# Layer 1 of a graph network: indices copied a group earlier, weights and a column row in PSUM, and a small POOL memset beside each gather

## What is computed

```python
def _L1_gnn_ref(x, W_u, b_u, W_v, src, dst):
    s_u = x @ W_u.T + b_u
    s_v = x @ W_v.T
    e = s_u[src] + s_v[dst]
    e = jnp.where(e >= 0, e, 0.2 * e)
    m = jax.ops.segment_max(e, dst, num_segments=n_nodes)
    e_exp = jnp.exp(e - m[dst])
    denom = jax.ops.segment_sum(e_exp, dst, num_segments=n_nodes)
    probs = e_exp / denom[dst]
    xh = x.reshape(n_nodes, head_dim, num_heads)
    msg = xh[src] * probs[:, None, :]
    out = jax.ops.segment_sum(msg, dst, num_segments=n_nodes)
    return out.reshape(n_nodes, dim)
...
x = _layernorm(x + _L0_gnn_ref(x, edge_index, edge_attr_64, ...), axis=-1)
x = _layernorm(x + _L1_gnn_ref(x, L1_gnn_W_u, L1_gnn_b_u, L1_gnn_W_v, src, dst), axis=-1)
```

## Time and profile before

| | us |
|---|---|
| median of three runs | 4930.07 |
| lowest, highest | 4929.89, 4938.38 |
| the profiled execution | 4929.81 |
| its span, first to last instruction | 4928.1 |

### The profile page before, as it was taken

One profiled execution on the slowest core, in us unless ns is written; L12 is line 12 of the kernel. 1 busy time (PEld: TensorE's weight loads), 2 busy tenths in 40 slices (PEclk: granted clock), 3 DMA queues, 4 the chain that ended last, 5 costly groups with the idle time before them and its releaser, 6 DMA issues. The chain is left out here.

```text
span 4928.1 us, 61408 instructions
## 1 busy us (share of the span) xinstructions
PE 3099.3 (63%) x13554; PEld 1900.6 (39%) x13555; DVE 2202.6 (45%) x5019; ACT 908.4 (18%) x2810; POOL 3434.9 (70%) x2948
## 2 busy tenths in 40 slices
PE   3547877777777777877778768834444444444441
PEld 1224444444444444444444435523333333333331
DVE  2543333333333333333333349855555555555554
ACT  0212222222222222222222223300000000000002
POOL 4238888888888888888888867756666666666564
PEclk9869898888998888888898889956666666666665
DMA  7777767667767677677677666643333333333332
GB/s 285 193 241 137 135 126 136 133 123 135 132 126 138 127 131 134 126 135 132 123 136 132 123 133 206 181 148 93 95 92 100 93 94 91 96 98 94 92 93 66
DMA packets 471760, 641.52 MB, mean 130 GB/s; under 512 B 173608, under 2 KB 365636, under 8 KB 467887
## 3 DMA queue, kind: packets, MB, share of 16 engines
q0 software_dynamic: 198144, 339.26, 36.4%
q1 hardware_dynamic: 245994, 254.83, 17.6%
q10 hardware_dynamic: 27588, 47.08, 3.0%
HBM read 448.23 MB, written 192.71 MB: 130 GB/s over the span
## 5 line engine op out<-in xcount | busy, mean ns | idle before, releaser
L935 POOL DMA_INDIRECT S<-l_msum,l_sink x784 | 1280.7, 1634 | 254.2 <-issue 213.5
L1466 POOL DMA_INDIRECT l_feats<-X_rows,l_gsrc x880 | 1008.1, 1146 | 605.6 <-DVE l_gsrc L1574 340.7
L918 POOL DMA_INDIRECT l_ga<-A_rows,l_gsrc x784 | 791.3, 1009 | 265.6 <-issue 155.4
L1008 PE MATMUL l_psU<-l_hid,l_same 128*128 128x257 f32 x1568 | 585.0, 458 | 534.7 <-ACT l_hid L1044 518.2
L981 PE MATMUL l_psC<-l_table,l_onehot 128*128 x4728 | 726.5, 295 | 0.0
L1532 PE MATMUL l_psU<-l_feats,l_same 128*128 128x264 f32 x1760 | 555.7, 481 | 146.5 <-DVE l_feats L1699 129.2
L1048 ACT COPY l_msum<-l_psU 128x257 f32<-128x257 f32 x784 | 292.6, 373 | 1883.8 <-POOLq L934 1296.1
L974 PE MATMUL l_psC<-W1cT,l_attrT 64*128 64x256 f32 x1576 | 619.0, 476 | 13.1 <-DMA l_table<-B_rows 13.1
L981 PEld LDWEIGHTS l_psC<-l_table,l_onehot 128*128 128x128 bf16 x4728 | 426.0, 104 | 364.9 <-issue 303.4
L1008 PEld LDWEIGHTS l_psU<-l_hid,l_same 128*128 128x128 f32 x1568 | 266.1, 213 | 669.9 <-ACT l_hid L1044 598.9
L1532 PEld LDWEIGHTS l_psU<-l_feats,l_same 128*128 128x128 f32 x1760 | 413.8, 242 | 281.8 <-issue 189.2
(11 more groups left out here) (346 smaller groups left out, 3512.2 us busy)
## 6 DMA issues: line engine op xcount, KB each, us to landing
l_srcb<-src_rows SPq DMA_DIRECT2D x99, 512.0 KB
l_locb<-lo_rows SPq DMA_DIRECT2D x55, 512.0 KB
S<-su_zeros ACTq DMA_DIRECT2D x24, 1156.5 KB
l_locb<-loc_rows SPq DMA_DIRECT2D x99, 256.0 KB
nd_sums<-S SPq DMA_DIRECT2D x196, 128.5 KB, 2.2
l_attr<-in_edge_attr SPq DMA_DIRECT2D x98, 256.0 KB
GH_rows<-l_hidden SPq DMA_DIRECT2D x49, 384.0 KB
nd_hidden<-GH_rows SPq DMA_DIRECT2D x49, 384.0 KB, 3.2
```

Of the source, the lines that this page charges most:

```text
L918: pool.indirect_dma_start(ga[:, s, :], None, D["A"], bass.IndirectOffsetOnAxis(ap=gsrc[h][:, j % HALF:j % HALF + 1], axis=0)).then_inc(gat ...
L935: pool.indirect_dma_start(D[f"S{j % NTAB}"], bass.IndirectOffsetOnAxis(ap=sink[j // HALF][:, j % HALF:j % HALF + 1], axis=0), msum[:, j % ...
L1008: nc.tensor.matmul(psU[j % 2][:, 0:UW], same[j // HALF][:, j % HALF, :], hid[:, j % RING, :], start=True, stop=True).then_inc(agg_done, 1)
L1466: pool.indirect_dma_start(feats[r][:, t, :], None, D["X1"], bass.IndirectOffsetOnAxis(ap=gsrc[r][:, t:t + 1], axis=0)).then_inc(gathered[r ...
```

## The change

- `stage_index(g + 2, r)` moves from the end of DVE's body g to its start.
- A new PSUM bank, `psW`, holds `weight` (128 columns) and `column` (128 columns). `K["column"]` is copied there once, ahead of the loop, and `find_edge` reads that copy.
- ACT takes the exponential of `below` twice: first into `weight` (`weights_ready`), then into `feats` as before (`weights_in_rows`). DVE multiplies by `weight`, and PE waits for `weights_in_rows` as well.
- POOL, in every body of `ahead` (53 groups), issues behind each gather a memset of the new tile `pause` (128 x 128 floats), which first waits for the memset before it.

```diff
--- before.py
+++ after.py
@@ -1383,11 +1383,13 @@
         goes_on = m.sb("goes_on", [P, XG])
         stays = m.sb("stays", [P, XG])
         xblock = m.sb("xblock", [1, XT])
+        pause = m.sb("pause", [P, P])
         word = m.sb("word", [1, XPACKED])
         words = m.sb("words", [1, XPACKED], I32)
         psE = m.ps("psE", [P, 512])
         psM = m.ps("psM", [P, 512])
         psV = m.ps("psV", [P, 512])
+        psW = m.ps("psW", [P, 512])
         psU = [m.ps(f"psU{q}", [P, 512]) for q in range(4)]
         keys_in, tables_ready, table_split = m.sem("keys_in"), m.sem("tables_ready"), m.sem("table_split")
         loc_in = [m.sem(f"loc_in{r}") for r in range(SETS)]
@@ -1399,12 +1401,15 @@
         ends_ready, ends_turned = m.sem("ends_ready"), m.sem("ends_turned")
         carries_ready, carries_turned, shrink_ready = m.sem("carries_ready"), m.sem("carries_turned"), m.sem("shrink_ready")
         max_ready, max_turned = m.sem("max_ready"), m.sem("max_turned")
-        below_ready, weights_ready = m.sem("below_ready"), m.sem("weights_ready")
+        below_ready, weights_ready, weights_in_rows = m.sem("below_ready"), m.sem("weights_ready"), m.sem("weights_in_rows")
         weighted, agg_done, acc_done = m.sem("weighted"), m.sem("agg_done"), m.sem("acc_done")
+        paused = m.sem("paused")
         dve_step, pool_waited = m.sem("dve_step"), m.sem("pool_waited")
         block = st.enter_context(nc.Block())
 
         ENDS, CARRY, SHRINK = P, P + 2 * GROUP, P
+        weight = psW[:, 0:GROUP * NH].rearrange("p (t h) -> p t h", h=NH)
+        column = psW[:, P:2 * P]
 
         def groups(engine, body):
 
@@ -1478,7 +1483,11 @@
                         pool.wait_ge(agg_done, g * PAIRS + (t + QUARTER) // PAIR)
                         pool.sem_inc(pool_waited, 1)
                     gather(r, t)
-
+                    pool.wait_ge(paused, g * GROUP + (t + 1))
+                    pool.sem_inc(pool_waited, 1)
+                    nc.gpsimd.memset(pause[:, :], 0.0).then_inc(paused, 1)
+
+            nc.gpsimd.memset(pause[:, :], 0.0).then_inc(paused, 1)
             ahead(pool, body)
             for r in range(SETS):
                 pool.wait_ge(gathered[r], 16 * GROUP * len(range(r, XG, SETS)))
@@ -1522,6 +1531,7 @@
                 pe.wait_ge(max_ready, g + 1)
                 nc.tensor.transpose(psM[:, 0:P], top[:, :], K["ident"][:, :]).then_inc(max_turned, 1)
                 pe.wait_ge(same_ready, g + 1)
+                pe.wait_ge(weights_in_rows, g + 1)
                 for n in range(PAIRS):
                     if n % 2 == 0:
                         pe.wait_ge(weighted, g * 4 + (n // 2 + 1))
@@ -1561,7 +1571,8 @@
                 act.wait_ge(carries_turned, g + 1)
                 nc.scalar.activation(shrink[:, :], psE[:, SHRINK:SHRINK + NH], ACT.Exp).then_inc(shrink_ready, 1)
                 act.wait_ge(below_ready, g + 1)
-                nc.scalar.activation(feats[r][:, :, H:XW], below[:, :, :], ACT.Exp).then_inc(weights_ready, 1)
+                nc.scalar.activation(weight, below[:, :, :], ACT.Exp).then_inc(weights_ready, 1)
+                nc.scalar.activation(feats[r][:, :, H:XW], below[:, :, :], ACT.Exp).then_inc(weights_in_rows, 1)
                 if not isinstance(g, int) or g < XG - SETS:
                     act.wait_ge(sv_done, g + 1)
                     stage_window(g + SETS, r)
@@ -1578,7 +1589,7 @@
                 nc.vector.tensor_scalar(onehot[:, :, :], locb[r][:, :, :], K["winid"][:, 0:1], None, ALU.is_equal).then_inc(onehot_ready, 1)
 
             def find_edge(g):
-                nc.vector.tensor_tensor(same[:, :, :], K["column"][:, :].unsqueeze(1).to_broadcast([P, GROUP, P]),
+                nc.vector.tensor_tensor(same[:, :, :], column.unsqueeze(1).to_broadcast([P, GROUP, P]),
                                         K["loX"][:, bass.ds(g * GROUP, GROUP)].unsqueeze(2).to_broadcast([P, GROUP, P]),
                                         ALU.is_equal).then_inc(same_ready, 1)
 
@@ -1627,6 +1638,7 @@
             split_float(nc, first_steps, K["svf"][:, :, :], svrest[:, :, :],
                         [table[:, :, n * NH:(n + 1) * NH] for n in range(NSPLIT)])
             dve.sem_inc(table_split, 1)
+            nc.vector.tensor_copy(column, K["column"][:, :])
             nc.vector.memset(ones[:, :], 1.0)
             nc.vector.memset(forth[:, 0:1], LOW)
             nc.vector.memset(carry[:, 1, GROUP - 1:GROUP], LOW)
@@ -1653,6 +1665,8 @@
                 c = Chain(dve, dve_step, base)
                 at = bass.ds(g * GROUP, GROUP)
 
+                if not isinstance(g, int) or g < XG - SETS:
+                    stage_index(g + SETS, r)
                 if not last:
                     find_node(g + 1, 1 - r)
                 if not first:
@@ -1693,9 +1707,8 @@
                     c.link(nc.vector.tensor_tensor(rows, rows, factor[:, :].unsqueeze(1).to_broadcast([P, XW // NH, NH]), ALU.mult))
                 dve.wait_ge(weights_ready, g + 1)
                 for q in range(4):
-                    f = feats[r][:, q * QUARTER:(q + 1) * QUARTER, :]
-                    f3 = f[:, :, 0:H].rearrange("p t (c h) -> p t c h", h=NH)
-                    w3 = f[:, :, H:XW].unsqueeze(2).to_broadcast([P, QUARTER, H // NH, NH])
+                    f3 = feats[r][:, q * QUARTER:(q + 1) * QUARTER, 0:H].rearrange("p t (c h) -> p t c h", h=NH)
+                    w3 = weight[:, q * QUARTER:(q + 1) * QUARTER, :].unsqueeze(2).to_broadcast([P, QUARTER, H // NH, NH])
                     nc.vector.tensor_tensor(f3, f3, w3, ALU.mult).then_inc(weighted, 1)
                     if q == 1 or q == 2:
                         add_sums(g, (2 * q - 2, 2 * q - 1), blocks, first)
@@ -1704,8 +1717,6 @@
                 if not last:
                     take_scores(g + 1, 1 - r, c)
                     local_max(g + 1, 1 - r, c)
-                if not isinstance(g, int) or g < XG - SETS:
-                    stage_index(g + SETS, r)
                 if first:
                     steps["first"] = c.n
                 elif "every" not in steps:
```

## The result

The changed kernel takes 4975.88 us, the median of 5 runs (4963.92 to 4982.53), against 4931.09 for the kernel before (5 runs). The ratio is 1.0083, with a 95% interval of 1.0065 to 1.0101: slower by 0.8%. Forecast were 4662 us, with 4570 to 4850 as the range.

What follows compares the result with a forecast made beforehand. The prediction took a ring of index list, gathers and scores, 28.97 us a group, to bound layer 1. Cut, POOL's 23.7 and DVE's 23.1 plus 0.3 jitter give 24.0 us, saving 268.4: 4662 us, range 4570 to 4850.

Steps and rivals of the forecast that it cites:

- The ring of index list, gathers and scores: Layer 1: POOL waits for DVE's index list, DVE for gathered rows, 28.97 us a group; copying a body earlier cuts it.
- the sum for the two chains and their jitter: Layer 1, per group: POOL 23.7 us, DVE 23.1, plus 0.3 for jitter passed between them, giving 24.0 us.
- The stretched gathers: POOL's gathers held up by DVE instructions with two SBUF inputs: 0.2 us each, 3.2 a group, of which about 0.5 stays.
- DVE's instructions on PSUM: DVE's `same` and weighting reading an operand in PSUM: priced at nothing, keeping 2.28 and 1.22 us.
- The memset: POOL, behind each of a group's 16 gathers: 0.20 us taken, between bounds of 0 and 0.50.
- The rival in which each gather starts anew: The memset and its wait empty POOL's sequencer, 0.92 us to each gather's start: 33.6 us a group, 5180 us; chance 0.08.
- the ring is cut, and what remains is the slower of two chains, POOL's and DVE's with PE: Layer 1 after the early index list: the slower chain sets the group time, POOL 23.7 us or DVE 23.1.
- DVE's chain: DVE with PE in layer 1, without the wait for gathered rows: 23.1 us a group.
- `agg_done` has come by the time POOL wants it: POOL between groups: sums of the group two before are finished before the next scores, so gathers run straight on.
- The rests that I struck from the bill: POOL's gathers: the surplus of 0.2 us each from stretching by DVE, of which 3.2 us a group shrinks to about 0.5.
- The rival on the far side of the sign: Slower than before: each gather starts anew behind its memset, 33.6 us a group, 5180 us; chance 0.08.

Runs made afterwards that it cites:

- h_reduces: b_index_only with DVE's edge-matrix comparison (all groups but the first) and weighting replaced by equally long reductions with one SBUF input, nothing in PSUM: 5017.37 us, ratio 1.0152.
- a_no_memset: The changed kernel without its memsets and their semaphore; early index list and PSUM operands stay: 5078.62 us, ratio 1.0282 to the kernel before.
- i_half_rows: a_no_memset with half the bytes in each gather (128 rows of 132 floats in place of 264): 5077.95 us, ratio 1.0291 to the kernel before.
- j_pause256: The changed kernel with memsets of 256 columns in place of 128: 4768.84 us, ratio 0.9662 to the kernel before.
- j_pause384: The changed kernel with memsets of 384 columns in place of 128: 4737.82 us, ratio 0.9603 to the kernel before.
- b_index_only: The kernel before with only the index list copy moved from the end of the body to its start: 4704.03 us, ratio 0.9515.
- l_every_second: b_index_only with a memset of 128 columns behind every second gather: 4665.59 us, ratio 0.9518, on a chip where the kernel before took 4901.51.
- c_psum_only: The kernel before with only weight and column in the new PSUM bank, index list late, no memset: 5142.47 us, ratio 1.0419.

## Why the prediction was wrong

- **The ring of index list, gathers and scores: right.** It bound the kernel, and the copy a body earlier cuts it. Alone it gives 24.66 us a group; the sum for the two chains and their jitter was 24.0 for the whole change.
- **The stretched gathers: right in cause and size.** They fell from 1146 to 969 ns, with 0.97 to 1.0 us forecast, and h_reduces shows the cause without PSUM: 958 ns as soon as DVE's long instructions have one SBUF input. The Trainium skill (SBUF — State Buffer, "Who interferes with whom") has VectorE instructions with two SBUF inputs collide with a GpSimd instruction that reads SBUF, and the trace agrees for this gather, which reads its index list `gsrc` there (1146 against 958 ns). Its inference that `tensor_tensor` does not stall a DMA's descriptor generation did not protect these gathers; but no run here separates the reading of the index list from the writing of descriptors, so the prediction went too far in taking the stretch as evidence against that inference.
- **DVE's instructions on PSUM: right.** 1216 and 2282 ns, against 1221 and 2282. "PSUM operands I price at nothing" holds for the instructions themselves.
- **The memset: too dear in the sum.** Gathers start 1.33 us apart, not 1.45. The gap of 0.30 shrinks to 0.17 behind a memset and the memset lasts 0.22, so it costs 0.09 net and not 0.20. The rival in which each gather starts anew was wrong as well.
- **The step that failed: "the ring is cut, and what remains is the slower of two chains, POOL's and DVE's with PE".** It took the two chains as independent, with 0.3 us for jitter. They are not: gathers at 1.25 to 1.33 us delay the signals on which DVE's chain runs. In the changed kernel the delay is 4.8 us at one wait of every group, and at the next it is 2.6 at the median where 0.43 stood before (from the end of the transposed maxima to L1702). DVE's chain, put at 23.1 us, then comes to some 30 (23.1 + 4.8 + 2.2), and 29.7 was measured. With it fell the step before it, that `agg_done` has come by the time POOL wants it ("It has"): POOL waited 397.9 us for PE's sums. The rests that I struck from the bill, 0.2 us a gather, were what kept the signals prompt. No rival had this. The rival on the far side of the sign had another mechanism and another price, 33.6 us a group, so that a slower kernel had a chance of 0.08 is no merit of it.
- **The parts do not add up.** Index list alone -4.8%, PSUM alone +4.2%, memset alone +0.5%: together they would give -0.1%, and +0.8% was measured. Plainer still, index list and PSUM would give -0.7% (from 0.9515 and 1.0419), and a_no_memset, which has both, is at +2.8%.

**A sign of it stood in the trace of before, under a wrong name.** At the start of layer 1 POOL sends the 32 gathers of groups 0 and 1 without a rest. The first scores wait 10.22 us, by the row until a DMA of the setup phase has landed; by the code they wait for the rows of group 0 and for `sv_done`, the signal of PE's L1494. In order of time, 3237 to 3262 us of the kernel before:

```profile
3237.62 10.84 DVE L1645 MEMSET acc<- 128x12936 f32 x1 [2.64 <-issue]
...
3241.43 0.58 PE L1494 MATMUL l_psV<-l_window,l_onehot 128*128 128x24 bf16 x16 [30.21 <-issue]
...
3254.46 0.95 POOL L1466 DMA_INDIRECT l_feats<-X_rows,l_gsrc  x1 [0.30 <-issue]
```

PE's products end at 3242.01, and their semaphore is recorded to change at 3258.55, 16.5 us later and 4.1 us after the start of the last of the 32 gathers. DVE, through with its memset at 3248.46, stands idle until then. Of the other 13 traces 12 show the same, with DVE idle for 9.0 to 11.4 us there. It is paid once and not in every group, so it cost the kernel before little; but it was the delay that decides the changed one.

## What to carry to other kernels

A wait that an edit removes may have been pacing something else, so ask what will now run at full rate, and try each part alone before all together: here one moved call was worth 4.8% and its companions more than ate it up. When a wait is longer than the work that it is for, compare two engines that wait for the same signal: if both start in the same instant, the signal was late and not the waiting engine. When the DMA or engine that a profile names as the releaser belongs to another phase, look in the code for the semaphore that is waited for. And a stretched instruction off the critical path is not a cost to be cleared away unless something waits for it.

## What the runs showed of the hardware

In this kernel, indirect DMAs of 128 rows that POOL sends 1.25 to 1.44 us apart, one after another, delay what PE signals, by up to 10.5 us at the carries' product (a_no_memset). It does so at a DMA load of 21 to 36% (i_half_rows 21, a_no_memset 31, the changed kernel 32, j_pause256 36, each from 4000 to 4200 us) and however few bytes each moves (i_half_rows). j_pause384 has the higher load, 38%, and none of the lateness. That the step lies near 1.5 us is a reading of the four kernels in the table, where 1.44 us still has 1.6 us of lateness and 1.55 has none; b_index_only shows 0.96 with stretched and unstretched gathers mixed.

How many gathers have gone before counts too. In the changed kernel 7 had been sent in a row when PE's product ended in the five groups that are on time, and 9 to 11 in the 25 late ones. In a_no_memset 24 of 28 signals come 3.6 to 4.1 us after the start of the group's last gather, with nothing sent in between: the delay lasts until POOL has stopped. The number alone does not decide it, for at the start of l_every_second a signal of PE is on time with 22 gathers sent, two of them stretched.

In a_no_memset, between 3400 and 4300 us, what goes out from DVE is on time: from the drop of the maxima to PE's product 0.05 us at the median and 0.06 at most (28 groups), from the maxima to PE's transposition 0.06 and 0.06, from `below` to ACT 0.03 and 0.04. The same is true of PE's signal for the turned scores, 0.04 at most, which comes some 5 us ahead of the late one.

The products themselves are not late, at least where several signals come together. In c_psum_only the semaphore of the sums is recorded to change at 4009.22, 4009.28 and 4009.34, for three pairs of tiles whose products are recorded to end at 4000.92, 4002.11 and 4003.00. Between 3400 and 4300 us 62 such changes come less than 0.3 us behind the one before; in the kernel before none comes less than 0.89 behind, which is the time from one pair to the next when PE works without a pause. Three pairs cannot be done in 0.12 us, so the work was done and its signals were held back.

What stays open is where they are held, and whether the single late signal of the carries is of the same kind: the ends of matmuls in the trace are modelled, and some semaphore changes are missing from it. Nor was it tried whether the number of gathers or the number of rows in them counts, since all gathers here have 128 rows.
